# State-space stage: side products spread one to a step, ScalarE's order around the exponential changed, one sum moved from VectorE to ScalarE

## The reference, cut to what matters

```python
normed = rmsnorm(x, input_norm_w)
xp = normed @ in_proj_W                       # 128 -> 512
x_z, z = xp[..., :256], xp[..., 256:]
xc = silu(conv(x_z, conv_W) + conv_b)          # 4 taps along the tokens
dt = clip(softplus(xc @ dt_W + dt_b), 0.001, 0.1)
Bp, Cp = xc @ B_W, xc @ C_W                    # 256 -> 64 each
A = -exp(A_log)                                # 64 numbers
def step(h, (x_t, dt_t, B_t, C_t)):            # h is 256 x 64 for each sequence
    h = exp(dt_t[..., None] * A) * h + dt_t[..., None] * B_t[:, None, :] * x_t[..., None]
    return h, einsum('ben,bn->be', h, C_t)
y = scan(step) * silu(z)
x = x + y @ out_proj_W                         # and a feed-forward part, another stage
```

## Time and profile before

| | |
|---|---|
| three runs | 6280.37, 6274.42, 6267.34 us, median 6274.42 |
| the profiled execution | 6281.87 us, its span 6280.2 us |
| mean granted clock of TensorE | 0.918 of full speed |
| busy over the span | PE 5088.8 us (81%), DVE 4814.6 us (77%), ACT 3339.4 us (53%), POOL 3326.7 us (53%) |
| L1839, once for each step 1 to 63 of 16 chunks | 1008 instructions, the first at 78.4 us, the last at 2302.4 us |

### The profile page before, as it was taken

One profiled execution on the slowest core, in us unless ns is written; L12 is line 12 of the kernel. 1 busy time (PEld: TensorE's weight loads), 2 busy tenths in 40 slices (PEclk: granted clock), 3 DMA queues, 4 the chain that ended last, 5 costly groups with the idle time before them and its releaser, 6 DMA issues. The chain is left out here.

```text
span 6280.2 us, 172165 instructions
## 1 busy us (share of the span) xinstructions
PE 5088.8 (81%) x62372; PEld 3018.0 (48%) x62372; DVE 4814.6 (77%) x8259; ACT 3339.4 (53%) x4888; POOL 3326.7 (53%) x3129
## 2 busy tenths in 40 slices
PE   6999999999999985886867966999967758887880
PEld 2444444444444333564655634666645546666440
DVE  5999999999999984897965355677759928888334
ACT  4666666666666653555741212444447627777440
POOL 4444454444444313665634573555547728877673
PEclk9999999999999997998979976999979959999995
DMA  1111111111111122221123641000011112222443
GB/s 47 51 45 51 48 47 47 49 44 50 47 48 48 43 58 77 54 56 35 43 69 89 141 118 44 17 17 18 14 29 38 32 52 64 62 63 56 154 141 108
DMA packets 610383, 363.38 MB, mean 58 GB/s; under 512 B 66217, under 2 KB 586732, under 8 KB 609772
## 3 DMA queue, kind: packets, MB, share of 16 engines
q1 hardware_dynamic: 588572, 328.56, 18.7%
q0 software_dynamic: 11648, 21.26, 1.8%
q10 hardware_dynamic: 9552, 5.58, 0.3%
HBM read 200.28 MB, written 66.85 MB: 43 GB/s over the span
## 5 line engine op out<-in xcount | busy, mean ns | idle before, releaser
L1409 ACT ACTIVATE mb_dA<-ps,mb_a_neg 128x1024 f32<-128x1024 f32 x1008 | 1124.1, 1115 | 788.6 <-PE ps L1167 787.8
L1845 DVE TENSOR_TENSOR mb_m<-mb_dA,ps 128x704 f32<-128x704 f32 x1008 | 892.7, 886 | 32.2
L1852 DVE TENSOR_TENSOR ps<-mb_m,ps 128x704 f32<-128x704 f32 x992 | 880.5, 888 | 0.1
L1150 PE MATMUL ps<-mb_m,mb_ident 128*32 128x320 f32 x7936 | 740.8, 445 | 7.2
L1199 PE MATMUL ps<-mb_m,mb_cz 128*32 128x256 f32 x8064 | 622.3, 380 | 31.2 <-issue 14.4
L1839 DVE TENSOR_TENSOR mb_m<-mb_dA,ps 128x320 f32<-128x320 f32 x1008 | 484.6, 481 | 84.8 <-PE ps L1150 65.9
L1182 PE MATMUL ps<-mb_ur,mb_bl 64*128 64x256 bf16 x4032 | 387.9, 271 | 49.5 <-DVE mb_m L1845 42.7
L1199 PEld LDWEIGHTS ps<-mb_m,mb_cz 128*32 128x32 f32 x8064 | 255.3, 110 | 324.0 <-issue 51.0
L1167 PE MATMUL ps<-mb_ur,mb_sel 64*128 64x256 bf16 x4032 | 396.3, 275 | 17.8 <-DMA mb_ur<-mb_pc 12.4
L1705 POOL TENSOR_TENSOR mb_ys<-mb_ys,mb_cbu 128x256 f32<-128x256 f32 x64 | 46.9, 733 | 531.5 <-ACT mb_ys L1506 530.6
L1167 PEld LDWEIGHTS ps<-mb_ur,mb_sel 64*128 64x128 bf16 x4032 | 114.9, 94 | 375.8 <-issue 251.2
(11 more groups left out here) (507 smaller groups left out, 13224.1 us busy)
## 6 DMA issues: line engine op xcount, KB each, us to landing
mb_ur<-mb_pc SPq DMA_DIRECT2D x768, 64.0 KB
mb_bl<-mb_pc SPq DMA_DIRECT2D x576, 64.0 KB
ef_w<-in_ef_w SPq DMA_DIRECT2D x35, 515.5 KB
mx_w<-in_mx_w SPq DMA_DIRECT2D x39, 384.0 KB
moe_made<-mx_y SPq DMA_DIRECT2D x39, 256.0 KB, 2.4
ea_wqk<-in_ea_wqk SPq DMA_DIRECT2D x70, 129.0 KB
ea_wvo<-in_ea_wvo SPq DMA_DIRECT2D x70, 128.5 KB, 2.2
ea_x<-hidden SPq DMA_DIRECT2D x280, 32.0 KB, 2.0
```

The source lines that it names most:

```text
L1150: mm = nc.tensor.matmul(out[c:c + 32], weights[:, c:c + 32], moving, start=start, stop=stop, skip_group_check=not grouped)
L1409: nc.scalar.activation(dA[:, t % RING].rearrange("p (g n) -> p g n", g=2), ps[:, DT:DT + 2, :], ACT.Exp, scale=a_neg[:, 0:1]).then_inc(dA_ ...
L1845: nc.vector.tensor_tensor(m[:, t % RING, DVE_PART], dA[:, t % RING, DVE_PART], state(u, t - 1, DVE_PART), ALU.mult).then_inc(md_ready.sem, 1)
L1852: nc.vector.tensor_tensor(h, m[:, t % RING, DVE_PART], h, ALU.add).then_inc(hd_ready.sem, 1)
```

## The change

Five things change. (1) `UT = [1, 2, 1, 1]`: `turn_u` and `project_bc`, and their copies, move one step later in block 1. (2) ScalarE runs `take_u` and `take_turn` ahead of the exponential of their step. (3) `gates` runs in tl 9 to 12 and its copies in tl 10 and 12; `project_c` runs once in each of tl 13, 14, 15 and 0. (4) In tl 0 of block 1 ScalarE runs `take_y` before `take_c`. (5) `weigh_bc` becomes an activation of ScalarE with an accumulated output, after the exponential of tl 11, and ahead of `take_dt` in block 3.

```diff
+    UT = [1, 2, 1, 1]
 # tensor, side()
-                    if tl == 1 and ahead:
+                    if tl == UT[j] and ahead:
-                    if tl == 2 and ahead:
+                    if tl == UT[j] + 1 and ahead:
-                            elif tl == 10:
+                            elif tl == 9:
                                 pe.wait_ge(xT_ready.sem, xT_ready.at(i + 2))
-                            if tl in (10, 11, 12, 13):
-                                gates(i + 2, tl - 10)
-                        if lead and tl == 14:
-                            if lead >= 2:
+                            if tl in (9, 10, 11, 12):
+                                gates(i + 2, tl - 9)
+                        if lead and tl >= 13:
+                            if lead >= 2 and tl == 13:
                                 pe.wait_ge(gates_taken.sem, gates_taken.at(i + 2))
-                            project_c(i + 1, 1 - u, 0)
-                            project_c(i + 1, 1 - u, 1)
-                        if lead and tl == 15:
-                            project_c(i + 1, 1 - u, 2)
+                            project_c(i + 1, 1 - u, tl - 13)
 # scalar
+                def weigh_bc(i, j):
+                    k = 4 * i + j
+                    act.wait_ge(cb_step.sem, cb_step.at(k))
+                    act.wait_ge(cbu_ready.sem, cbu_ready.at(k - 1))
+                    nc.scalar.activation(cb_prod[:], cb_prod[:], ACT.Identity, accum_out=cb[:, 0:1]).then_inc(cb_ready.sem, 1)
 # scalar, chunk(), in each step
+                        if j == 0 and lead >= 2 and tl == 8:
+                            take_turn(i + 2)
+                        ip, jp = (i, j + 2) if j < 2 else (i + 1, j - 2)
+                        if tl == UT[j] and (j < 2 or lead):
+                            take_u(ip, jp)
                         if t + 3 < T:
                             decay(i, t + 3)
 ...
-                        if j == 1 and tl == 0 and lead:
-                            take_c(i + 1, 1 - u)
                         if tl == 0 and behind:
                             ... take_y
+                        if j == 1 and tl == 0 and lead:
+                            take_c(i + 1, 1 - u)
 ...
-                            if tl == 1:
-                                take_u(ip, jp)
-                            elif tl == 2:
+                            if tl == UT[j] + 1:
                                 take_bc(ip, jp)
 ...
+                            elif tl == 11:
+                                weigh_bc(ip, jp)
-                            if tl == 8:
-                                take_turn(i + 2)
-                            elif tl in (11, 13):
-                                take_gates(i + 2, (tl - 11) // 2)
+                            if tl in (10, 12):
+                                take_gates(i + 2, (tl - 10) // 2)
 # vector
-                def weigh_bc(i, j):
-                    ...
-                    nc.vector.tensor_reduce(cb[:], cb_prod[:], AX.X, ALU.add).then_inc(cb_ready.sem, 1)
-                        if tl == 11:
-                            if j < 2:
-                                weigh_bc(i, j + 2)
-                            elif lead:
-                                weigh_bc(i + 1, j - 2)
```

More of the change, by code:

```diff
@@ L1545, in first @@
                         round_mid(0, j)
+                        weigh_bc(0, j)
                     decay(0, 1)
@@ L1567, in chunk @@
                                 take_y(i, j - 1)
+                        if j == 1 and tl == 0 and lead:
+                            take_c(i + 1, 1 - u)
                         if j < 2 or lead:
-                            ip, jp = (i, j + 2) if j < 2 else (i + 1, j - 2)
-                            if tl == 1:
-                                take_u(ip, jp)
-                            elif tl == 2:
+                            if tl == UT[j] + 1:
                                 take_bc(ip, jp)
@@ L1824, in split_lo @@
                         lo_ready.sem, 1)
-                def weigh_bc(i, j):
-                    k = 4 * i + j
-                    dve.wait_ge(cb_step.sem, cb_step.at(k))
-                    dve.wait_ge(cbu_ready.sem, cbu_ready.at(k - 1))
-                    nc.vector.tensor_reduce(cb[:], cb_prod[:], AX.X, ALU.add).then_inc(cb_ready.sem, 1)
                 def decay_pe_part(i, u, t):
@@ L1874, in first @@
                     split_lo(0)
-                    weigh_bc(0, 0)
                     own_rows(1)
@@ L1878, in first @@
                     split_lo(1)
-                    weigh_bc(0, 1)
                     gate_x(1)
```

## The result

The changed kernel takes 6238.8 us (median of five runs, 6234.7 to 6246.3); the kernel before takes 6274.4 (median of five, 6264.8 to 6282.1). The ratio is 0.9946, with a 95% interval of 0.9931 to 0.9961. The forecast was 6239. Single runs lie up to 10 us from their medians, so that agreement is luck in the last digits; the intervals inside a chunk, which repeat to 0.01 us, are what the steps are judged by.

The account below looks back on a forecast made before the run. VectorE's back-to-back products set the plain step of 2.12 to 2.13 us; stalls over it can be won. Terms of -2.21 us a full chunk, -35.4 in all, took the 6274.42 median to 6239; range 6220 to 6264.

Parts of the forecast that it names:

- The account of lateness: TensorE's add may start up to 1.31 us after L1839; eight matmuls give back 0.04, a copy wait adds 0.54.
- Part 1: Blocks 0, 2 and 3: `take_u` ahead of the exponential ends `project_bc`'s wait, 0.23 each, -0.69 us a chunk.
- Part 2: Block 0, turned copies first and products spread: stall of 0.52 turns into 0.64, +0.12 us a chunk; spreading wins nothing.
- Part 3: Block 1, y copy first and `turn_u` later: stalls of 0.38 in place of 1.87, -1.49 us a chunk.
- Part 4: Sum moved from VectorE to ScalarE: -0.39 us a chunk in blocks 0 to 2, +0.24 in block 3.
- the prediction's account of the border: Block 3 to the next chunk: TensorE and ScalarE set the pace, first exponentials follow each other; L1839 of step 2 waits 1.09.
- The run-in: Before the chunks, where VectorE makes the sum only after `split_lo`, with the next `turn_u` behind it: -0.9 us.
- A: Rival, block 0: turned copies cost nothing, L1167 of step 9 doesn't wait for exponential 11; 6230 us, chance 0.13.
- B: Rival, block 1 keeps its stall: `contract` waits for something besides the y copy, or `turn_y` waits; 6256 us, chance 0.17.
- C: Rival, no measurable change: block 3's sum costs 0.49, block 0's delay doubles, block 1 keeps its stall; 6265 us, chance 0.09.
- D: Rival, slower: the sum doesn't fit ScalarE's gap, needing function table loads each time; about 6363 us, chance 0.03.
- the sign by which I wanted to know D: ScalarE's idle time before its exponentials falling by more than 60 us beyond the shorter stage would show D.

Follow-up runs that it names:

- e2: Changed kernel with the two turned-block copies behind the exponential of step 8 again: chunk 136.69 us, whole time 6250.5 us.
- e4: Changed kernel with the two gate copies also ahead of the exponential: chunk 134.82 us, whole time 6220.1 us.
- e7: Changed kernel with the first dt copy (step 59) ahead of its exponential: chunk 135.19 us, whole time 6265.0 us (kernel before beside it 6307.3).
- e8: Changed kernel with gate copies, y copies of blocks 0 to 2 and first dt copy ahead of the exponential: chunk 134.20 us, 6254.0 us, 0.9914 of kernel before.
- e3: Changed kernel with the copy of u behind the exponential again in all blocks: chunk 136.99 us, whole time 6251.5 us.
- e9: Changed kernel with block 0's spreading undone (gates in steps 10 to 13, two products in step 14): chunk 136.45 us, whole time 6251.8 us.
- e1: Changed kernel with the sum back on VectorE: chunk 135.80 us, whole time 6243.1 us.
- e5: Changed kernel with the C copy before the y copy again in step 16: chunk 136.23 us, whole time 6276.9 us (kernel before beside it 6307.3).
- e10: The kernel of e8 with the sum back on VectorE: chunk 134.75 us, whole time 6229.5 us (kernel before beside it 6282.3).
- e11: Kernel before with only the sum moved to ScalarE, ahead of the gate and dt copies: chunk 138.22 us, whole time 6270.4 us (kernel before 6282.3).

## Why the prediction came out right

**The account of lateness.** The step that carried the forecast, 1.31 as the limit, 0.04 given back in a step with eight matmuls, 0.54 added by a wait behind the exponential, was right. It gave the two new stalls to 0.02, and its results in e2, e4, e7 and e8 came to within 0.1 us a chunk. It was 0.2 short in e3 and 0.3 in e9, in both by the place or the length of a wait that it had not followed.

**Part 1** was right: 0.22 in each of three blocks, and in the waits `take_u` no longer ends one of `project_bc` inside the chunks. e3 shows that the copy's place is worth more in the changed kernel (1.25), since block 1 has no slack left to hide the wait.

**Part 2** was right in size: 0.62 in place of 0.52, forecast 0.64. The sentence behind it, that spreading wins nothing here, was too broad. It was true of the sum of the edits in block 0. But against the alternative with the turned copies ahead and the products doubled, the spreading saves 0.70 (e9).

**Part 3** was right: 0.34 in place of 1.87, forecast 0.38; the 0.03 in step 20 did not show.

**Part 4** had the price right and its credit wrong. The accumulated sum took 0.247 and 0.191 and put the copy behind it 0.23 later (490.13 - 489.90, ScalarE's rows below), forecast 0.24. ScalarE's groups and step 59 of chunk 2 in the kernel after:

```profile
L1492 ACT ACTIVATE mb_cb_prod<-mb_cb_prod 128x64 f32<-128x64 f32 x64 | 15.8, 247 | 0.0
...
L1492 ACT ACTIVATION_READ_ACCUMULATOR mb_cb_prod<-mb_cb_prod 128x1 f32 x64 | 12.2, 191 | 0.0
```

```profile
489.90 0.24 ACT L1492 ACTIVATE mb_cb_prod<-mb_cb_prod 128x64 f32<-128x64 f32 x1
490.04 0.19 ACT L1492 ACTIVATION_READ_ACCUMULATOR mb_cb_prod<-mb_cb_prod 128x1 f32 x1
490.13 0.68 ACT L1460 ACTIVATE mb_ex<-ps,mb_dt_b 128x512 f32<-128x512 f32 x1
```

But I booked 0.13 of block 0 to the sum, in a block in which TensorE sets the pace one step later. e1 shows it hidden there: with the sum on VectorE step 12 loses nothing, without it 0.14. Part 2 had reckoned with plain steps, so its 0.14 in step 12 holds the same 0.13 as a cost; the total is right (-2.21 a chunk, measured -2.24), but the sum's own share is not. As booked, it was a gain of 0.15 a chunk; measured by taking it back, 0.05.

The price in block 3 was right, its sign in the waits less so. TensorE's wait for the first dt copy, in step 60, grew from 0.29 to 0.65, where about 0.5 was forecast:

```profile
490.86 0.64 PE L1151 MATMUL ps<-mb_xz,mb_w_dt 128*32 128x256 f32 x8 [0.65 <-ACT mb_ex L1460]
```

The 0.36 more are the sum's 0.23 and the 0.13 that VectorE no longer loses ahead of it. And the prediction's account of the border, that the first exponentials of the next chunk follow each other and set the pace, was not the main thing: e7 moves one dt copy and takes 0.55 of the 0.60, more than the 0.35 by which it had grown.

**The run-in** was wrong: 0.9 forecast, nothing to be seen. The first L1840 starts at 78.2 us, before at 78.4, and the first piece's transfer had been issued 0.26 earlier already (60.99 against 61.25 us). `turn_u` did come earlier, but the steps wait for the pieces, and SyncE's queue issues these one after another from 61 us on. In the kernel after its timeline begins so, and TensorE's first products wait for the pieces:

```profile
60.99 0.64 SPq L1100 DMA_DIRECT2D mb_ur<-mb_pc  x1
61.68 0.62 SPq L1101 DMA_DIRECT2D mb_bl<-mb_pc  x1
62.35 0.59 SPq L1100 DMA_DIRECT2D mb_ur<-mb_pc  x1
```

```profile
76.42 0.61 PE L1168 MATMUL ps<-mb_ur,mb_sel 64*128 64x256 bf16 x4 [13.04 <-DMA mb_ur<-mb_pc]
```

The scan gained 33.8 where 34.5 (35.4 less the run-in) was forecast for it.

**The rivals.** A fell: exponential 11 does hold L1168 of step 9. B fell: e5 shows that `contract` waits for the y copy. C fell: the sum's price was 0.23 and not 0.49, and the interval of the ratio lies clear of 1. D fell: the stage still has a single table load (the last row below), e10 and e8 differ by the sum alone, and the kernel with it on ScalarE has the shorter chunks. But the sign by which I wanted to know D was badly chosen. ScalarE's idle time before its exponentials went from 788.6 to 674.9 us, 114 less, 80 beyond the 34 of the shorter scan, where I had set 60 as the alarm. It went to the front of the copies that now run first. ScalarE's groups in the kernel after:

```profile
L1407 ACT ACTIVATE mb_dA<-ps,mb_a_neg 128x1024 f32<-128x1024 f32 x1008 | 1123.6, 1115 | 674.9 <-PE ps L1168 667.6 <-DVE mb_m L1846 6.4
...
L1468 ACT COPY mb_tm<-ps 128x512 f32<-128x512 f32 x64 | 37.6, 588 | 58.8 <-PE ps L1254 57.2 <-POOL mb_cbu L1693 1.6
...
L1421 ACT ACTIVATE mb_xT_tok<-ps,mb_norm_w 128x512 f32<-128x512 f32 x16 | 11.0, 687 | 8.1 <-PE ps L1208 8.0
...
L1414 ACT ACT_TABLE_LOAD x1 | 1.3, 1283 | 3.0 <-PEq L69 3.0
```

58.8 and 8.1, of which there was next to nothing before (2.6 and 0.1), and 64 sums of 0.23, 15 us, make the 80.

For the rule of the Trainium skill (ScalarE: Activation LUTs, "Rules for kernel authors") that adds belong on VectorE the answer is both: in the kernel before it holds (e11, 0.23 a chunk lost by leaving it), with the copies in order it does not (e10, 0.55 won by leaving it). On the price alone the trace agrees with the rule: the sum took VectorE 0.211 us and takes ScalarE 0.247 and 0.191. The 7 us of loss that the prediction worked out from the rule did not come, since the sum moved to an engine that had idle time there.

## What to carry to other kernels

Where engines run their work in a fixed order, count how late the second engine may be without being felt, and follow this lateness step by step; a gain on one engine in front of a stall that another sets is no gain. A copy that another engine waits for belongs ahead of a long operation whose result is needed only steps later: the long one comes later by about the copy's duration (0.58 to 0.62 us here) and by what the copy itself waits for its input (0.50 in e7), and the copy no longer waits for the whole of the long one. Before moving a small operation to an idle engine, look at what stands behind it in that step: the same sum was a loss, nothing and a gain in three orders of the same kernel.

## What the runs showed of the hardware

The next operation of ScalarE can start before a copy's recorded end: the turned copies took 0.69 and 0.70, and the next operation started 0.58 and 0.59 after each; the y copy took 0.36 and the next started 0.25 later. SyncE issued the 42 transfers of the first pieces 0.63 to 0.69 us apart, but for two gaps of 0.88 and 1.04. The kernel before took 6281.0 and 6282.3 beside two groups of kernels and 6307.3 beside a third. The kernels of the third group (e5 to e8) took some 30 us more behind the scan, while the intervals inside a chunk that their edits leave alone were the same as in the other groups to 0.01 us. Why is not known.
